# A feed-forward layer with eight experts: all experts for every token, or the two chosen ones on sorted tokens

## The reference

```
x = x + tanh(g_ffn) * ffn(layernorm(x))
ffn(x):  scores = sigmoid(x @ router.T)             # 8 experts in 2 groups of 4
         group  = the group whose two best (scores + bias) sum higher
         two    = the two best experts of that group
         w      = scores[two] / (sum of scores[two] + 1e-20)
         routed = sum over e in two of  w[e] * ((silu(x @ w_gate[e]) * (x @ w_up[e])) @ w_down[e])
         shared = (silu(x @ sw_gate) * (x @ sw_up)) @ sw_down
         return routed + shared
```

## Time and profile before

| what | us |
|---|---|
| median of 3 runs (1168.93 to 1169.73) | 1168.97 |
| the profiled execution, first to last instruction | 1167.4 |
| TensorE products busy in it | 1137.5 |
| VectorE, ScalarE, GpSimd busy | 859.4, 647.0, 383.2 |
| feed-forward block, from 814.7 | 352.7 |

### The profile page before, as it was taken

The page is one execution under the profiler, slowest core; times in us unless marked ns, Lnnn a source line. Parts: engine busy times, 40 slices in busy tenths (PEclk is TensorE's granted clock), DMA queues, the critical chain, the costliest instruction groups (busy, mean ns, idle before and its releaser), DMA issues. The chain is left out here.

```text
span 1167.4 us, 26523 instructions
## 1 busy us (share of the span) xinstructions
PE 1137.5 (97%) x8481; PEld 1095.4 (94%) x8481; DVE 859.4 (74%) x2059; ACT 647.0 (55%) x1561; POOL 383.2 (33%) x577
## 2 busy tenths in 40 slices
PE   5899999999999999999999999998999999999998
PEld 4899999999999999999999999997999999999998
DVE  5777777777777777777777777776876767767766
ACT  4766566666656666566666666655433333333333
POOL 2512112122121221212212121211366666666663
PEclk9999999999999999999999999999899999999999
DMA  9300000000000000000000000000112121121121
GB/s 298 112 15 5 0 3 3 0 3 0 3 1 1 3 0 3 0 3 3 0 3 0 3 3 0 0 1 1 37 47 83 47 75 60 50 85 45 54 84 64
DMA packets 23861, 34.92 MB, mean 30 GB/s; under 512 B 3744, under 2 KB 20240, under 8 KB 21776
## 3 DMA queue, kind: packets, MB, share of 16 engines
q1 hardware_dynamic: 23536, 34.33, 8.7%
q10 hardware_dynamic: 288, 0.13, 0.0%
HBM read 30.13 MB, written 4.33 MB: 30 GB/s over the span
## 5 line engine op out<-in xcount | busy, mean ns | idle before, releaser
L245 POOL TENSOR_TENSOR prob<-prob,rinv 128x333 f32<-128x333 f32 x128 | 94.6, 739 | 617.7 <-DVE rinv L474 617.7
L450 DVE TENSOR_REDUCE nmax<-ps_s 128x1 f32<-128x333 f32 x256 | 127.6, 499 | 65.6 <-PE ps_s L548 65.5
L320 ACT ACTIVATE prob<-ps_s,nmax 128x333 f32<-128x333 f32 x256 | 137.3, 536 | 63.8 <-DVE nmax L450 62.3
L904 ACT ACTIVATE th<-ps_gu 128x256 f32<-128x256 f32 x144 | 55.3, 384 | 211.8 <-PE ps_gu L1165 211.8
L1165 PE MATMUL ps_gu<-xt_hi,gu_hi 128*128 128x256 f32 x576 | 164.7, 286 | 1.8 <-DVE xt_lo L962 1.6
L1165 PE MATMUL ps_gu<-xt_lo,gu_hi 128*128 128x256 f32 x576 | 164.0, 285 | 0.0
L1165 PE MATMUL ps_gu<-xt_hi,gu_lo 128*128 128x256 f32 x576 | 164.0, 285 | 0.0
L430 DVE SCALAR_TENSOR_TENSOR k_lo<-ps_k,vecs,k_hi 128x334 fp32r<-128x334 f32 x128 | 72.5, 566 | 82.7 <-ACT k_hi L302 82.7
L330 ACT ACTIVATE o_hi<-ps_qa,vecs 128x256 fp32r<-128x256 f32 x127 | 60.4, 475 | 131.1 <-PE ps_qa L548 131.1
L857 POOL TENSOR_TENSOR f_lo<-act_h,f_hi 128x256 fp32r<-128x256 f32 x131 | 97.0, 741 | 107.3 <-ACT f_hi L898 107.3
L1085 DVE SCALAR_TENSOR_TENSOR act_a<-th,ps_gu 128x256 f32<-128x256 f32 x144 | 60.0, 417 | 87.1 <-ACT th L904 87.0
(11 more groups left out here) (162 smaller groups left out, 3652.2 us busy)
## 6 DMA issues: line engine op xcount, KB each, us to landing
wide_w<-comb_rows SPq DMA_DIRECT2D x16, 1024.0 KB, 4.6
out_dram<-y_out SPq DMA_DIRECT2D x16, 256.0 KB, 2.1
x_all<-in_x_dram SPq DMA_DIRECT2D x1, 3584.0 KB, 17.4
raw<-in_L_xattn_Wkv_dram SPq DMA_DIRECT2D x4, 512.0 KB, 7.1
ctx_in<-in_ctx_dram SPq DMA_DIRECT2D x16, 77.0 KB
raw<-in_L_xattn_Wq_dram SPq DMA_DIRECT2D x2, 512.0 KB, 7.0
raw<-in_L_xattn_Wo_dram SPq DMA_DIRECT2D x2, 512.0 KB, 10.3
raw<-in_L_ffn_w_gate_dram SPq DMA_DIRECT2D x4, 256.0 KB, 4.4
```

What stands on the lines that cost most here:

```text
L245: pool.tensor_tensor(prob[:, h % 2, 0, 0:KEYS], prob[:, h % 2, 0, 0:KEYS], rinv[:, h % 2, 0:1].to_broadcast([P, KEYS]), ALU.mult).then_inc ...
L320: act.activation(prob[:, h % 2, i, 0:KEYS], ps_s[i][:, 0:KEYS], ACT.Exp, bias=nmax[:, h % 2, i:i + 1], accum_out=rsum[:, h % 2, i:i + 1]). ...
L450: dve.tensor_reduce(nmax[:, h % 2, i:i + 1], ps_s[i][:, 0:KEYS], AX.X, ALU.max, negate=True).then_inc(max_ready, 1)
```

## The change

The feed-forward block is written anew as `sparse_ffn`, fully unrolled, in two passes; `x2_statistics`, `x2_aggregate` and `x2_keep` move its statistics into attention, each one step after the other, behind the batch's last update.

- Pass A goes over 16 duos (two tiles). ScalarE normalises, TensorE computes the shared expert and the router's logits in one bank (widths 272, 256, 272), and VectorE writes the residual with the shared part. Every 8 tiles (a chunk) VectorE chooses each token's experts in 19 steps (`routing`), of which two are run at each of three places in a duo; TensorE's `count` adds up how many tokens went to each expert, and with that each token gets a row number in each of two lists, by its first and by its second expert. GpSimd then sends the rows to DRAM by indirect DMAs, 128 rows each: `by_first` (normalised row, residual, weights and addresses, 2064 bytes a row) and `by_second` (1040 bytes). 24 tiles have slots in SBUF.
- A table of 40 tiles per list is computed: which expert a tile has and where it begins.
- Pass B goes over 80 tiles in 40 duos: SP fetches a tile's sorted rows at an address read from the table, TensorE runs gate, up and down with the tile's expert, whose weights are addressed by a register (`bass.ds(e, 1)`), VectorE multiplies by the weight and adds the earlier sum, and GpSimd sends the rows by an indirect DMA: for the first list to `half_done`, in the place that the row has in the second list; for the second to the output. Between the lists SP waits for all rows of the first.
- Silu is ScalarE's own function, followed by one multiplication on VectorE.

The core of the diff, added lines:

```
+            def x2_statistics(b):
+                for i in range(TT):
+                    dve.bn_stats(stats2[:, i, :], latents(b, i)).then_inc(bn2_ready, 1)
...
+            def fetch(tile):
+                rank_no, j = divmod(tile, XTILES)
+                s = tile % NB
+                if tile >= NB:
+                    sp.wait_ge(e_y, tile - NB + 1)
+                    sp.wait_ge(e_to, tile - NB + 1)
+                start = sp.value_load(tab_row[0:1, rank_no * HALF + j:rank_no * HALF + j + 1], min_val=0,
+                                      max_val=EXP * REGION - P)
+                if rank_no == 0:
+                    sp.dma_start(xin[:, s, :], d0[bass.ds(start, P), :]).then_inc(row_in[s], 16)
+                else:
+                    sp.dma_start(xin[:, s, 0:ROW1], d1[bass.ds(start, P), :]).then_inc(row_in[s], 16)
+                return start
...
+                sp.wait_ge(sent[c], 16 * RANKS * CHUNK)
+            sp.wait_ge(tab_ready, 1)
+            for tile in range(XTILES):
+                fetch(tile)
+            held = [(tile, fetch(tile)) for tile in range(XTILES, XTILES + NB)]
+            for s in range(NY):
+                sp.wait_ge(y_sent[s], 16 * len(range(s, XTILES, NY)))
+            for tile, start in held:
+                fetch_sum(tile, start)
+            for tile in range(XTILES + NB, RANKS * XTILES):
+                fetch_sum(tile, fetch(tile))
...
+            def send(c):
+                pool.wait_ge(route, ROUTE * (c + 1))
+                pool.wait_ge(id_placed, c + 1)
+                pool.wait_ge(z_ready, CHUNK * (c + 1))
+                for k in (1, 0):
+                    width, region = ((ROW0, d0), (ROW1, d1))[k]
+                    for tile in range(c * CHUNK, (c + 1) * CHUNK):
+                        if k == 0:
+                            pool.wait_ge(resid_ready, tile // TT + 1)
+                        pool.indirect_dma_start(region[:, :], bass.IndirectOffsetOnAxis(ap=dest[:, tile, k:k + 1], axis=0),
+                                                rows[:, slot(tile), 0:width], None, bounds_check=EXP * REGION - 1,
...
+            def address(tile):
+                rank_no, j = divmod(tile, XTILES)
+                s, y = tile % NB, tile % NY
+                pool.wait_ge(row_in[s], 16 * uses(tile, NB))
+                if tile >= NY:
+                    pool.wait_ge(y_sent[y], 16 * (tile // NY))
+                col = rank_no * HALF + j
+                pool.tensor_scalar(to_row[:, y:y + 1], xin[:, s, 3 - rank_no:4 - rank_no], skip[:, col:col + 1], None,
...
+            def send_row(tile):
+                rank_no = tile // XTILES
+                y = tile % NY
+                region, limit = ((acc, EXP * REGION - 1), (out, ROWS - 1))[rank_no]
+                pool.wait_ge(e_to, tile + 1)
+                pool.wait_ge(e_y, tile + 1)
+                pool.indirect_dma_start(region[:, :], bass.IndirectOffsetOnAxis(ap=to_row[:, y:y + 1], axis=0), yout[:, y, :],
+                                        None, bounds_check=limit, oob_is_err=False).then_inc(y_sent[y], 16)
...
+                address(tile)
+            for tile in range(RANKS * XTILES):
+                send_row(tile)
+                if tile + 4 < RANKS * XTILES:
+                    address(tile + 4)
...
+            def gate(d):
+                act.wait_ge(gu_done, TT * (d + 1))
+                if d >= 1:
+                    act.wait_ge(h_done, d)
+                c = d // CDUOS
+                if c >= 2:
+                    act.wait_ge(logits_ready, c - 1)
+                at = TT * (d % CDUOS)
+                act.activation(lparts[:, c % 2, at:at + TT, :], ps_g[:, :, 2 * I:SHW], ACT.Copy).then_inc(parts_ready, 1)
+                act.activation(silu[:, :, :], ps_g[:, :, 0:I], ACT.Silu).then_inc(silu_done, 1)
...
+            for d in range(DUOS + 2):
+                if d + 2 < DUOS:
+                    normalise(TT * (d + 2))
+                    normalise(TT * (d + 2) + 1)
+                if d + 1 < DUOS:
+                    tokens_hi(d + 1)
+                if d >= 1 and d % CDUOS == 0 and d <= DUOS:
+                    logit_gate(d // CDUOS - 1)
+                if 0 <= d - 1 < DUOS:
+                    hidden_hi(d - 1)
+                if d < DUOS:
+                    gate(d)
+                for n in W_AT.get(d, ()):
+                    split_hi(n)
...
+            def hidden(d):
+                dve.wait_ge(parts_ready, d + 1)
+                dve.wait_ge(silu_done, d + 1)
+                if d >= 2:
+                    dve.wait_ge(h_turned, d - 1)
+                dve.tensor_tensor(act_h[:, d % 2, :, :], silu[:, :, :], ps_g[:, :, I:2 * I], ALU.mult).then_inc(h_done, 1)
...
+                    tokens_lo(d + 1)
+                steps(2)
+                if d < DUOS:
+                    hidden(d)
+                steps(2)
+                if 0 <= d - 1 < DUOS:
+                    hidden_lo(d - 1)
+                steps(2)
+                if d >= 2:
+                    residual(d - 2)
...
+            def e_output(n):
+                dve.wait_ge(e_down, n + 1)
...
+                    s, y = tile % NB, tile % NY
+                    if rank_no == 0:
+                        dve.wait_ge(row_in[s], 16 * uses(tile, NB))
+                    else:
+                        dve.wait_ge(acc_in[s], 16 * (uses(tile, NB) - len(range(s, XTILES, NB))))
+                    if tile >= NY:
+                        dve.wait_ge(y_sent[y], 16 * (tile // NY))
+                    dve.scalar_tensor_tensor(out=yout[:, y, :], in0=ps_o[:, n % 2, i * DIM:(i + 1) * DIM],
+                                             scalar=xin[:, s, rank_no:rank_no + 1], in1=xin[:, s, ROW1:ROW0],
+                                             op0=ALU.mult, op1=ALU.add).then_inc(e_y, 1)
...
+            def shared_gate_up(d):
+                pe.wait_ge(xtlo_ready, d + 1)
+                if d == 0:
+                    pe.wait_ge(shlo_ready, 2)
+                else:
+                    pe.wait_ge(h_done, d)
+                    pe.wait_ge(parts_ready, d)
+                for i in range(TT):
+                    n = 0
                     for c in range(FC):
+                        at = c * TOK + i * P
+                        for x, w, width in ((xt_hi, sh_hi, SHW), (xt_hi, sh_lo, 2 * I), (xt_lo, sh_hi, SHW)):
+                            mm = pe.matmul(ps_g[:, i, 0:width], x[:, d % 2, at:at + P], w[:, c, 0:width],
+                                           start=n == 0, stop=n == 3 * FC - 1, skip_group_check=True)
+                            n += 1
...
+            for d in range(DUOS + 2):
+                if d + 1 < DUOS:
+                    turn_tokens(d + 1)
+                if d < DUOS:
+                    shared_gate_up(d)
+                if 0 <= d - 1 < DUOS:
+                    turn_hidden(d - 1)
+                if d >= 2:
+                    shared_down(d - 2)
+                if d >= CDUOS + 1 and (d - CDUOS - 1) % CDUOS == 1:
+                    count((d - CDUOS - 1) // CDUOS)
+            count(CHUNKS - 1)
...
+            def expert(tile):
+                rank_no, j = divmod(tile, XTILES)
+                at = P + rank_no * HALF + j
+                return pe.value_load(tab_row[0:1, at:at + 1], min_val=0, max_val=EXP - 1)
...
+            def e_gate_up(n, which):
+                pe.wait_ge(e_xtlo, n + 1)
+                if n >= 2:
+                    pe.wait_ge(e_h, n - 1)
+                for i in range(TT):
+                    e = which[i]
+                    k = 0
                     for c in range(FC):
+                        at = c * TOK + i * P
+                        for x, w in ((xt_hi, gu_hi), (xt_hi, gu_lo), (xt_lo, gu_hi)):
+                            mm = pe.matmul(ps_g[:, n % 2, i * TOK:(i + 1) * TOK], x[:, n % 2, at:at + P],
+                                           w[:, c, bass.ds(e, 1), :].rearrange("p o n -> p (o n)"), start=k == 0, stop=k == 3 * FC - 1)
+                            k += 1
+                mm.then_inc(e_gu, 1)
...
+            def e_down_part(n, which):
+                pe.wait_ge(e_htlo, n + 1)
+                if n >= 2:
+                    pe.wait_ge(e_y, TT * (n - 1))
                 for i in range(TT):
...
+                    for k, (h, w) in enumerate(((ht_hi, dn_hi), (ht_hi, dn_lo), (ht_lo, dn_hi))):
+                        mm = pe.matmul(ps_o[:, n % 2, i * DIM:(i + 1) * DIM], h[:, n % 2, i * P:(i + 1) * P],
+                                       w[:, bass.ds(which[i], 1), :].rearrange("p o n -> p (o n)"), start=k == 0, stop=k == 2)
+                mm.then_inc(e_down, 1)
...
+                if n < XDUOS:
+                    known[n] = [expert(TT * n + i) for i in range(TT)]
+                if n + 1 < XDUOS:
+                    e_turn_tokens(n + 1)
+                if n < XDUOS:
+                    e_gate_up(n, known[n])
+                if 0 <= n - 1 < XDUOS:
+                    e_turn_hidden(n - 1)
```

(2 more changed lines are left out.)

1050 lines of the change are left out of this document (595 added, 455 removed).

## The result

The changed kernel took 1137.61 us (median of 4 runs, 1137.03 to 1137.79) beside 1169.35 of the kernel before: ratio 0.9729, interval 0.9715 to 0.9743. Faster, as forecast, and inside the range, but the gain is 31.7 us where 68 were forecast. And this measurement was itself off its kind: three later measurements of the same instructions gave 1123.7, 1122.4 and 1124.0 (ratios 0.9624, 0.9608, 0.9611). So there are two questions: why about 22 us were missed in every case, and what 14 more were in the first.

What follows compares the result with a forecast made beforehand. TensorE was taken to pace attention and feed-forward; afterwards GpSimd's sends decide. Block 1.3 + 136 (pass A) + 147 (pass B with fill) = 284, from 814.7 to 1099, plus 1.6: 1101 us; range 1045 to 1200.

Steps and rivals of the forecast that it cites:

- a send's price: GpSimd's queue, both passes: time per indirect DMA of 128 rows, taken as 1.4 us, the middle between 0.37 and 2.5.
- the change of rank: Pass B between the lists: SP waits until all first-list sums have landed before fetching them, 6 us.
- GpSimd's period in pass B: Per tile a send of 1.4 us and addresses of 0.2; 3.2 us a duo, setting pass B's pace.
- Rivals 2 and 4: Dear sends, both passes: 1187 us at 2.0, 1259 at 2.5 (chance 0.13); TensorE at half clock in B: 1177 us (0.05).
- the first rank: Pass B over the list by first expert, 40 tiles: its sends were forecast at 64 us.
- Between: From pass A's last send to pass B's first: landing 3 us and filling B's pipe 8, together 11.
- the way to the first send: Start of the feed-forward block until the first chunk is routed, with attention's added 1.3 us: 36.3 us.
- the end: End of the program: the last send and its landing, 5 us.
- the second rank: Pass B over the list by second expert, 40 tiles: its sends were forecast at 64 us.
- the prediction's formula: Feed-forward block time as 82.7 us plus 144 times a send's price; equal to the old block at 1.87 us.
- this slack hides: Pass A: tiles 24 to 31 wait for the first chunk's sends to free slots; claimed covered, costing nothing.
- Rival 3: TensorE's sequencer in pass B: register loads and register-held weight addresses slow it, 1163 us, or 1239 at worst (chance 0.16).

Runs made afterwards that it cites:

- first measurement: The changed kernel as written, measured first beside the kernel before: 1137.61 us, ratio 0.9729.
- third measurement: The changed kernel again with the very same text, nothing edited: 1122.4 us, ratio 0.9608; its profiled span is 1120.9.
- the later wait: The changed kernel with ScalarE normalising tiles 24 to 31 one turn of its loop later, so the wait for slots comes later: 1118.8 us, ratio 0.9572.

## Why the prediction was right and wrong

Right: the sign; that TensorE's products stop being the question, in pass A at least; attention at 1.3 us (1.4, 1.9, 2.7 and 1.6 in the four measurements); a send's price within its bounds and on the cheap side (1.28 for 1.4); the change of rank (5 for 6); GpSimd's period in pass B (1.57 us a tile for 1.6); no switch of ScalarE's tables in the sum (one load, none after it). Rivals 2 and 4 fell: no send near 1.87, and TensorE's clock at 1.00 through the first rank. The Trainium skill, DMA: Bandwidth & Descriptors, Latency and other measured facts, gives about 1 us to the first byte of a DMA issued by GpSimd and lays it to the software that writes the descriptors. What was measured here is another quantity, the time that a send holds GpSimd's queue; it lies near that figure, at 0.97 to 1.06 us for 128 rows and 0.88 for 16.

The gain in the first measurement fell short by some 36 us. Of these 14 are that measurement's own, and no step of the prediction could have had them. The other 22 are terms of the sum, third measurement against forecast: Between +9.0, the way to the first send +5.6, the end +4.5, the second rank +3.9, the first rank +1.5, the change of rank -1.1, the sends of pass A -1.5. That it is only 22 is partly luck: with the measured price of a send the prediction's formula gives 814.7 + 267 + 1.6 = 1083 us, 39 under the third measurement.

The step that failed, and by the most, is the one called "Between": the pipe of B fills in 8 us, so 11 with the landing. It measured 20.0 to 21.3. Its terms were summed along one pair as if nothing stood between, but TensorE's queue has the second pair's turn ahead of the first gate-and-up, and two more pairs' gate-and-up ahead of the first down product. Timeline of TensorE, third measurement:

```profile
960.47 1.09 PE L1481 MATMUL ps_x<-ident,rows 128*128 128x128 f32 x4 [32.73 <-DMA rows<-by_first]
...
963.47 0.56 PE L1500 MATMUL ps_g<-gu_hi,xt_hi 128*128 x1
...
966.35 0.36 PE L1500 MATMUL ps_g<-gu_hi,xt_hi 128*128 x1
...
968.86 0.36 PE L1500 MATMUL ps_g<-gu_hi,xt_hi 128*128 x1
...
970.51 0.36 PE L1519 MATMUL ps_o<-dn_hi,ht_hi 128*128 x1
```

Ten us from the first turn to the first down product and 2.5 more to the send (973.00); ahead of them 2.1 for the landing, 3.9 for the first fetch with its register load, where 3 were set, and 1.4 until the pair's second tile is there. About 1 us of the ten goes with the clock: after 32.7 us in which TensorE stood idle it was granted at 0.50 (1.2 GHz) from 960 to 965 us, and the first run of 12 gate-and-up products takes 2.40 us from its first start to its last, the third run 1.39. All this was read from the order in the code and the trace, not tried with another order.

Next, the end: 5 us were set for the last send and its landing, 10.5 are there from its start. The landing is 2 of them; the rest is GpSimd's DRAIN, which the sum did not have at all. No row shown of the kernel before has GpSimd's queue being closed, and I gave it no bound from above.

Third, the way to the first send: 36.3 forecast, 41.9 in the third measurement. Of the 5.6 us, 1.4 come with attention's later end (2.7 for 1.3) and 3.4 with the first pair. The first Silu stands at 827.79 there, 10.4 us after the block's start, where my sum has about 7: the power on 8 columns takes 1.64 us, not the 0.70 of two columns, and the table load of 1.28 us stands in the first pair, where nothing covers it.

Fourth, "this slack hides": in pass A I counted the slot wait as covered because the engines need only 76 us in all. Slack over a stage covers a wait only if what is queued behind it is not due earlier. Here ScalarE's wait for tiles 24 to 31 stood ahead of the pairs between whose steps chunk 1's routing is finished, and GpSimd paid 4.3 us, of which the later wait gave back 2.8. In pass A the sends came 7.3 us cheaper than forecast (82.3 for 89.6) and what stands between the chunks 5.8 dearer (14.2 for 8.4); the two nearly cancel, which is why 96.5 looks like 98. Nor were TensorE and VectorE done with pass A as early as the 76 us say: TensorE stood idle for 33 us ahead of pass B, where some 50 were forecast.

Rival 3 was right in mechanism and I had priced it as all or nothing. A register load costs 0.47 us (0.5 was its assumption), two a pair; the address in a register costs a product nothing (0.12 us from start to start, as with fixed addresses). Together the loads add 0.5 us to the 2.77 of a pair without them, which puts TensorE at 3.2 to 3.3, level with GpSimd's 3.15. That is why the sum's 3.2 us came true although, with cheaper sends, it should have fallen to 2 x (1.28 + 0.2) = 3.0, and why relieving GpSimd alone gained nothing: the number was right by luck. In the second rank SP is a third bound at the same height, one that I had called covered: its 1.67 us a tile can't win back the lead that it loses at the change of rank.

Two slips in the working did not move the sum. The parts given for TensorE's pair, 2.15 + 0.66 + 0.38 less 0.7, make 2.49 and not 2.85; the measured 2.77 lies near the number and not near its parts. And rival 4's 1177 us is slower than the kernel before, so its 0.05 belonged under slower and not under faster.

Last, the 14 us between the first measurement and the others: no term of the forecast could have had them, and the table only places them: 6.9 us in pass A, where GpSimd waits 8.27 us for chunk 2 (0.17 in the third), 4.2 in the first rank, under 2 anywhere else.

Of Silu I said that it gains nothing alone; in the nine-expert kernel it gains 6.9 us, a fifth of what the whole change gained in the first measurement. How much it gives inside the sorted form was not tried.

## What to carry to other kernels

Price a new pipeline's fill by walking the slowest queue in its written order up to the first output, not along one item; and ask of every wait what is queued behind it, since a stage's slack belongs to the last item only. When several queues come within some 6% of each other, relieving one gains little: look for the second and third bound before the edit, and for every place where a queue that runs ahead has to stop, since its lead may not come back. Count products in a window rather than trust a busy share of 97%. And measure the unchanged kernel again beside its variants: here one odd measurement would have credited every variant with 14 us that its edit did not make.
